# A transformer block with 16 routed experts: the experts run on tokens sorted by expert instead of on every token

## What is computed

```python
probs = softmax(xt @ w_router)              # 2048 tokens, 16 experts
top_w, top_i = top_k(probs, 4)              # 4 experts per token
top_w = top_w / sum(top_w)
cw = zeros(T, E).at[t, top_i].add(top_w)    # 0 for the other 12 experts
g = silu(xt @ we1[e]) * (xt @ we3[e])       # 256 -> 128, for each expert e
moe_out = sum_e (g * cw[:, e]) @ we2[e]     # 128 -> 256
shared = silu(xt @ ws1) * (xt @ ws3) @ ws2  # 256 -> 512 -> 256, every token
out = shared / 5 + moe_out * 4 / 5
```

## Time and profile before

| | us |
|---|---|
| median of 3 runs (lowest, highest) | 907.44 (905.76, 910.16) |
| the profiled execution's own time | 905.22 |
| its span from first to last instruction | 903.5 |
| span of the first block (attention) | 543.2 |
| span of the second block (feed-forward) | 360.3 |

### The profile page before, as it was taken

One profiled execution on the slowest core, in us unless ns is written; L12 is line 12 of the kernel. 1 busy time (PEld: TensorE's weight loads), 2 busy tenths in 40 slices (PEclk: granted clock), 3 DMA queues, 4 the chain that ended last, 5 costly groups with the idle time before them and its releaser, 6 DMA issues. The chain is left out here.

```text
span 903.5 us, 14599 instructions
## 1 busy us (share of the span) xinstructions
PE 831.8 (92%) x5552; PEld 538.9 (60%) x5552; DVE 662.6 (73%) x1061; ACT 433.6 (48%) x630; POOL 190.1 (21%) x250
## 2 busy tenths in 40 slices
PE   8579699999999999999998978699999999999996
PEld 6245344344444444444443557588888888888885
DVE  7457888789999999989954546777567657666675
ACT  3221287777777777777876423122322232222221
POOL 6200112222222222133311327840100010001001
PEclk9879599999999999999999978799999999999999
DMA  6757024443333333344300204410000000000000
GB/s 193 185 112 215 3 54 96 86 111 92 92 92 81 88 83 84 82 127 131 81 27 13 76 1 120 124 38 1 24 1 1 1 24 0 1 1 24 1 1 23
DMA packets 42789, 58.51 MB, mean 65 GB/s; under 512 B 11044, under 2 KB 30564, under 8 KB 40612
## 3 DMA queue, kind: packets, MB, share of 16 engines
q1 hardware_dynamic: 42068, 57.02, 23.9%
q10 hardware_dynamic: 656, 0.59, 0.4%
HBM read 39.21 MB, written 17.96 MB: 63 GB/s over the span
## 5 line engine op out<-in xcount | busy, mean ns | idle before, releaser
L617 ACT ACTIVATE probs<-psum 128x1024 f32<-128x1024 f32 (+3 forms) x384 | 289.6, 816 | 124.4 <-PE psum L802 122.2
L1022 DVE TENSOR_REDUCE max_parts<-psum 128x8 f32<-128x1024 f32 (+2 forms) x192 | 235.3, 1226 | 59.5 <-PE psum L776 55.9
L1200 ACT ACTIVATE mid<-psum 128x512 f32<-128x512 f32 x80 | 47.8, 597 | 251.5 <-PE psum L1223 238.0
L816 PE MATMUL psum<-probs,v_aug 128*32 128x512 f32 (+3 forms) x1536 | 166.7, 507 | 0.4 <-POOL probs L498 0.3
L802 PE MATMUL psum<-qs,ks 64*128 64x512 f32 (+3 forms) x768 | 156.9, 408 | 4.9 <-ACT probs L617 4.7
L802 PEld LDWEIGHTS psum<-qs,ks 64*128 64x128 f32 x768 | 73.2, 188 | 128.9 <-ACT probs L617 113.4
L498 POOL TENSOR_SCALAR_AFFINE_SELECT probs<-probs 128x512 f32<-128x512 f32 x128 | 81.2, 635 | 260.9 <-ACT probs L617 260.9
L1315 DVE TENSOR_TENSOR mid<-mid,psum 128x512 f32<-128x512 f32 x80 | 55.0, 688 | 107.7 <-ACT mid L1200 107.7
L1029 DVE TENSOR_REDUCE max_parts<-psum 128x1 f32<-128x512 f32 x192 | 130.7, 681 | 0.0
L776 PE MATMUL psum<-km,qs 64*128 64x128 f32 (+2 forms) x704 | 93.8, 338 | 33.3 <-DMA km<-k_parts 22.6
L1301 DVE SCALAR_TENSOR_TENSOR acc<-psum,wo_sb,acc 128x256 f32<-128x256 f32 x240 | 99.2, 476 | 0.0
(11 more groups left out here) (141 smaller groups left out, 959.9 us busy)
## 6 DMA issues: line engine op xcount, KB each, us to landing
km<-k_parts SPq DMA_DIRECT2D x62, 160.0 KB
y_sums<-g_sign SPq DMA_DIRECT2D x32, 256.0 KB, 3.0
qs<-q_parts SPq DMA_DIRECT2D x62, 128.0 KB
wl_raw<-in_L_ffn_we_dram SPq DMA_DIRECT2D x36, 128.0 KB, 2.3
ks<-k_parts SPq DMA_DIRECT2D x64, 64.0 KB
x_sb<-in_L_attn_x_dram SPq DMA_DIRECT2D x4, 512.0 KB, 7.2
q_parts<-w_hi SPq DMA_DIRECT2D x8, 256.0 KB, 5.5
q_parts<-w_lo SPq DMA_DIRECT2D x8, 256.0 KB, 3.1
```

Source lines behind the costliest of these rows:

```text
L617: act.activation(probs[:, s % (LAG + 1), 2 * hh:2 * hh + 2, off:TT], psum[:, 2 * hh:2 * hh + 2, off:TT], ACT.Exp, scale=SCALE).then_inc(p_ ...
L816: last = pe.matmul(bank[sum_bank][32 * h:32 * h + 32, off:TT], v_aug[:, group, c, :], probs[:, s % (LAG + 1), h, off:TT], start=(c == 0), ...
L1022: dve.tensor_reduce(out=max_parts[:, :, h0:h1, slice(*tiles), slot], in_=psum[:, wide_bank:wide_bank + 2, :].rearrange("p a (s w) -> p (a ...
```

## The change

**Routing makes a sorted order.** For each batch, DVE finds the four best experts of each token (`best`, `chosen`), PE counts with a triangular matrix of ones how many tokens of each expert come before a token (`ranks`, 16 small matmuls), and DVE computes at which row of a sorted list each of the 4096 (token, expert) pairs belongs (`firsts`, `places`). Every expert's rows begin at a multiple of 128, so 47 tiles of 128 rows (`TILES = T * TOPK // P + E - 1`) hold any distribution; `experts` gives the expert of each tile. Two batches make NTILE = 94.

**POOL moves the rows.** `sort(b)` issues 32 indirect DMAs, each of which scatters 128 normalised rows of 1 KB to their places in DRAM (`xs[b]`); `gather(b)` issues 32 more which fetch the four results of 128 tokens each (8 token tiles x 4) from `ys[b]`. The gathers have two buffers of four tiles (NG = 2). Padding rows must be zero: during attention groups 2 to 9, POOL issues eight DMAs of 12 (or 11) x 128 rows of zeros, at step 6.

**The routed experts run tile by tile.** SP loads tile i and stores the result of tile i - 8. PE transposes the tile (2 transposes), does 6 matmuls of 256 moving columns with the expert's weights, whose address comes from a register (loaded from SBUF for 4 tiles at a time), transposes the product (1), and does 3 matmuls with W2. ACT scales and shifts (2 instructions), takes the Silu, the high part, and copies every other result out; DVE has product, high part and low part of the activations, low part of the product, and the other copies. These are laid out in iterations: in iteration i PE does up of tile i+1, the transposes of tile i+3, down of tile i-2, the transpose of the product of tile i.

**The shared expert stays dense.** `shared(t)` is a pass of four experts over 512 tokens; LEAD = 3 passes run in front of the tiles and one behind. Its order is up(e), down(e - 1), and `g_hi`/`g_lo` have one buffer.

**Combination.** `combine(n)` on DVE adds the four weighted results of a token tile to x: 6 instructions of 256 columns. The first batch's eight run inside the tile loop, every fourth tile from tile 55; the second batch's eight run in the last shared pass, two for each of its four experts.

**Weights.** All 16 experts are loaded by 20 DMAs at the start of the second block (6.3 MB); the high parts are made by ACT (L1406 of the new file, 768 columns) and the low parts by DVE, two experts for each of the eight experts of the first two shared passes. The four experts that were prepared during attention are now the shared one's.

**In the attention block** the first batch's norm, transposes and router come two steps earlier, its routing is done there (`best` and `chosen` between the two reciprocals of DVE, `ranks` before the second batch's transposes, the rest at the end), and the second batch's two low parts move from POOL to DVE.

The diff, cut to its core (the routing class is described above):

```diff
-        w_hi = sb(whole, "w_hi", [P, NEARLY, WCOLS], F32R)
-        w_lo = sb(whole, "w_lo", [P, NEARLY, WCOLS], F32R)
+        w_hi = sb(whole, "w_hi", [P, NS, WCOLS], F32R)
+        w_lo = sb(whole, "w_lo", [P, NS, WCOLS], F32R)
...
+                        if s == 6 and 2 <= group < 2 + 4 * B:
+                            b, part = (group - 2) // 4, (group - 2) % 4
+                            at = slice(12 * part, min(12 * part + 12, TILES))
+                            pool.dma_start(xs[b].rearrange("(a p) d -> p a d", p=P)[:, at, :],
+                                           zeros.unsqueeze(1).to_broadcast([P, at.stop - at.start, D])).then_inc(zero_out, 16)
...
+                def sort(b):
+                    pool.wait_ge(pos_ready, b + 1)
+                    pool.wait_ge(zero_out, 16 * 4 * B)
+                    for j in range(TC):
+                        for r in range(TOPK):
+                            k = j * TOPK + r
+                            pool.indirect_dma_start(out=xs[b], out_offset=bass.IndirectOffsetOnAxis(ap=posi[:, b, k:k + 1], axis=0),
+                                                    in_=xn2[b][:, j // TJ, j % TJ, :], in_offset=None).then_inc(sorted_s[b], 16)
+
+                def gather(b):
+                    stored(pool, (b + 1) * TILES)
+                    if b == 0:
+                        pool.wait_ge(sorted_s[1], 16 * ROUTES)
+                    for j in range(TC):
+                        n = b * TC + j
+                        if n >= NG:
+                            pool.wait_ge(combined, n - NG + 1)
+                        for r in range(TOPK):
+                            k = j * TOPK + r
+                            pool.indirect_dma_start(out=rows[:, n % NG, r, :], out_offset=None, in_=ys[b],
+                                                    in_offset=bass.IndirectOffsetOnAxis(ap=posi[:, b, k:k + 1], axis=0))\
+                                .then_inc(rows_in_s[n % NG], 16)
+
+                sort(0)
+                sort(1)
+                gather(0)
+                gather(1)
...
-                        if e >= 2:
-                            down(e - 2)
-                    down(NE - 2)
-                    down(NE - 1)
+                        if e:
+                            down(e - 1)
+                    down(NS - 1)
...
+                for i in range(-AHEAD_T, NTILE + BEHIND_Y):
+                    if 0 <= i + 1 < NTILE:
+                        up_rows(i + 1)
+                    if i + AHEAD_T < NTILE:
+                        turned_rows(i + AHEAD_T)
+                    if i >= BEHIND_Y:
+                        down_rows(i - BEHIND_Y)
+                    if 0 <= i < NTILE:
+                        turned_g(i)
+                    if i == RANK_AT:
+                        route[1].ranks(pe, bank[RANK_BANK])
+                for t in range(LEAD, NPASS):
+                    shared(t)
```

More of the change, by code:

```diff
@@ L1096, in _ @@
                     dve.reciprocal(l32[:, toks], l32[:, toks]).then_inc(r32_done, 1)
+                    if half == 0:
+                        route[0].best(dve, chain.link)
+                        route[0].chosen(dve, chain.link)
                     dve.wait_ge(y_in[2 + half], 32)
@@ new lines, in _ @@
+                for t in range(LEAD):
+                    shared(t)
+                for i in range(-AHEAD_T, NTILE + BEHIND_Y):
+                    if 0 <= i + 1 < NTILE:
+                        product(i + 1)
+                    if i + AHEAD_T < NTILE:
+                        split_x(i + AHEAD_T)
+                    if 0 <= i < NTILE:
+                        low_rows(i)
+                    if i >= BEHIND_Y and (i - BEHIND_Y) % 2 == 0:
+                        products_out(i - BEHIND_Y)
+                    if i == RANK_AT - 10:
+                        route[1].best(dve, link)
+                    elif i == RANK_AT - 6:
+                        route[1].chosen(dve, link)
+                    elif i == RANK_AT + 3:
+                        route[1].firsts(dve, link, bank[RANK_BANK])
+                    elif i == RANK_AT + 5:
+                        route[1].places(dve, link)
+                    elif i == RANK_AT + 7:
+                        route[1].experts(dve, link)
+                    if i >= FIRST_COMBINE and (i - FIRST_COMBINE) % 4 == 0 and (i - FIRST_COMBINE) // 4 < TC:
+                        combine((i - FIRST_COMBINE) // 4)
```

612 lines of the change are left out of this document (423 added, 189 removed).

## The result

The changed kernel takes 913.73 us (median of 12 runs, 909.62 to 920.37) beside 907.82 for the kernel before (12 runs, 904.2 to 912.38). The ratio is 1.0063, 95% interval [1.0035, 1.009]: slower by 0.6%, where 890 us and a gain were forecast.

The account below looks back on a forecast made before the run. PE was taken to bound the second block, computing 16 experts where each token needs 4. 543.2 + 2 (A) + 79.4 (B) + 208 (C) + 54.5 (D) = 887 us of span, + 1.7 = 889, stated as 890; range 852 to 938.

Parts of the forecast that it names:

- Step A: Attention block: zero fills hidden on POOL, first routing ends late, `ranks` and `places` in existing waits; +2 us (0 to +10).
- Step B: Three shared passes before the tiles: 74.4 us plus 5 for the first round's weights and reduced clock, 79.4 us.
- The 2.17 us: Shared passes: PE's wait before a down, for Silu, product and low part, now coming in every round.
- a pass is 24.8 us: One shared pass, including three waits of 2.17 us before a down; 16.7 us without the waits.
- Step C: Loop over 94 tiles: DVE 194 us as likely bound, 10 for mutual waiting, 4 for filling; 208 us.
- Step D: Tail after the last tile: 32 gathers on POOL, last combination, down, additions, output; 16 + 32c, 54 us.
- c: POOL's time for one indirect transfer of 128 rows; taken as 1.2 us, between 0.47 and 2.3.
- Rival 1: POOL's transfers set the end, from c = 1.7 on: 918 us at c = 1.8, 946 at 2.3; chance 0.17.
- Rival 2: PE becomes the loop's bound with a falling clock: +35 us in loop, +8 in shared passes, 932 us; chance 0.17.
- Rival 3: Zero fills stop the attention block, at 14.4 us of POOL each: +32 us, 921 us; chance 0.08.
- Rival 4: Everything overlaps well: c = 0.8 and 2.0 us per tile, 858 us; chance 0.12.
- 337 + 15 + 11 us: Second block of the kernel before: four passes 337 us, 15 lost at the start, 11 at the end; given as 360.3.

Follow-up runs that it names:

- f1: The changed kernel run again with nothing changed, with a second profile: 913.6 us, ratio 1.010 to the kernel before.
- f3: Changed kernel with `best`, `chosen` behind both y_t products and `firsts`, `places`, `experts` behind h2_lo: 920.3 us, 1.015 of the kernel before.
- g2: Changed kernel with only `chosen` moved, behind the first y_t product: 989.9 us, 1.088 of the kernel before, in a slow (kind 2) series.
- f4: Changed kernel with each of the eight zero fills issued twice: 919.5 us, 1.015 of the kernel before.
- i3: Changed kernel, shared passes reordered: ACT's high part of e-1 before Silu of e, DVE's low part before the product: 898.1 us, 0.988 of before.
- i4: Changed kernel with LEAD = 2, high parts first, second routing five tiles earlier, `chosen` later, combinations in three pieces: 876.8 us, 0.964 of before.
- kind 1: Label for series at the faster level, like the result on record: the unchanged changed kernel takes 913.6 us there, 1.010 of the kernel before.
- kind 2: Label for series at the slower level: the unchanged changed kernel takes 986.3 us there, 1.083 of the kernel before.
- j1: Changed kernel with POOL's indirect transfers replaced by plain ones of the same bytes at fixed rows, kind 2: 904.7 us, 0.995 of before.

## Why the prediction was wrong

The forecast was 890 us, faster at 0.58; it came out slower by 0.6%, inside the range and on the side that had 0.35. The step that failed most is B, the three shared passes: 79.4 us forecast, 89.6 in f1 and 93.1 in the profiled execution. It had no term for the lower clock behind a wait and none for what DVE does between the last pass and the first tile. A, C and D slipped by 3.5 to 4.6 us each in f1. The sum of the slips, 23 us there, is larger than the gain of 16 that was left.

- **Step A, "+2 us (0 to +10)".** Two terms failed. "It ends late: +2" is 5.2 and 5.0 us in the two profiles: the 8.43 us for which DVE waited ended at its product, and the routing cannot start before the logits, so it came behind that hole, not into it, and part of it was held up beside POOL. "`ranks` and `places` lie in waits that were there anyway" is wrong for DVE: f3 and g2 moved the work about and got nothing. "A fill of up to 10 us costs nothing": on POOL a fill takes 1.08 us, not 5.6, but a second set of fills cost some 6 us in f4, by a way that stays open.
- **Step B, "79 us".** The 2.17 us were right (2.01), and so was pass 0 within 2 us in f1 (31.7 for 29.8; 35.2 in the profiled execution). What failed is "a pass is 24.8 us": it takes 27.0. From the first down to the second of pass 1 in f1 it is 8.0 us, to the third 6.5, for a forecast of 6.35: behind the first wait of a pass, the down and part of the next up run at the lower clock. One down of 1.43 us is 1.68 behind a wait at the full clock and up to 2.9 where the clock has fallen; i3, with most of the waits gone, has PE busy 1.7 us less for the same pass. Missing altogether: 3.9 us between the last pass and the loop's first L1530, of which 3.3 are PE's wait for DVE's four additions and the split of the first tile. The four additions are in step D's sum and were put at nothing here. 1.9 + 2.2 + 2.2 + 3.9 = 10.2 us. No edit took those 3.9 us away; they are read from the timeline.
- **Step C, "208 us".** 211.5 without the store, near the forecast, but partly by luck. DVE's operations cost what was worked out, 1.50 us per tile, and yet DVE is busy 154 us of the loop and not 194, for the recorded durations overlap a little where gaps had been added; PE has 176 us, 1.87 per tile, for which "near 1.9" was right. So DVE was not the bound, and 38 us of waiting on top of PE's work stand where 10 on top of DVE's were forecast. The slow stretch is made by combinations in one piece, 2.8 us during which PE waits 2.0 us, at a granted clock of 0.83 for the stretch. i4 shows it. The stop for `sort(1)`, named as a danger, is there, some 3 us.
- **Step D, "54 us".** c was taken as 1.2 and is 1.26, 1.31 with the waits for the two row buffers: +3.7 us in f1; the last down ran at the lower clock, 2.9 us for 1.6. The fit of the Trainium skill that was weighed there (DMA: Bandwidth & Descriptors, Anatomy of one DMA), 2.3 us, would have been wrong if read as time on POOL; as latency it is near for a gather, which lands 2.8 us after issue, and low for a scatter, 4.8.
- **Rival 1** (POOL sets the end, c above 1.7): not so on kind 1. On kind 2 its result, 8% slower, is there at an unchanged c, by a mechanism that the prediction doesn't name: others stand still while POOL works.
- **Rival 2** (falling clock): the mechanism is true, its price was given too high; it is spread over B (27.0 for 24.8 us a pass), C (clock 0.83 for 62 us) and D (the last down). "Waits of 2.2 us" were given as a reason against it, and behind the first wait of 2.0 us of a pass the lower level was there. The forecast should have carried part of it, not left it to a rival.
- **Rival 3** (fills stop the attention): no, a fill holds POOL for 1.08 us. **Rival 4** (everything overlaps): no.
- Two sums of the prediction don't come out, and neither moves the forecast. 337 + 15 + 11 us are 363 and not 360.3; the start loses 12.6 us, not 15 (the second block's first pass ends at 640.0). And at c = 1.8 `sort(1)` would cost 5 us more by the sum given, not 9.

## What to carry to other kernels

When a change takes work from an engine that was never idle, price the new stage as if it ran partly at the lower clock: in these passes 7.5 us of waits cost themselves and 1.7 to 2.2 us again. Write down for every seam between two stages what each engine still has to do of the old one: the 3.9 us at the loop's start were in nobody's list. Look at the order of an engine that only passes things on (here ACT) before adding buffers: one exchanged pair of calls on ACT and one on DVE were worth 15 us. And measure a kernel with indirect transfers in more than one series before believing half a per cent.

## What was not expected of the hardware

- Two levels by series, 914 and 986 us for one program, 905 to 908 for the kernel before in all; j1 ties it to indirect transfers.
- A plain transfer of 128 rows takes POOL 0.54 us, an indirect one 0.96 + 0.30, a fill of 1536 rows 1.08.
- DVE's operations on few elements, beside a tensor operation of POOL: 1.64 us for 0.19, 2.96 for 0.90, the first ending with POOL's operation.
- Zero fills (12 MB in all) raise the DMA share from 0.38 to 0.49 (120 to 420 us), and issuing each twice makes the kernel 5.9 us slower, though neither POOL nor the waits for loads in the trace account for it.
